# Adding the four quadrants' column sums of a softmax: with six DMAs inside SBUF and VectorE in place of a product on TensorE

## The reference

```python
x_q = einsum('oc,bcn->bno', w_qk, y)
x_k = einsum('oc,bcn->bon', w_qk, x)
x_v = einsum('oc,bcn->bon', w_v, x) + b_v
energy = einsum('bnc,bcm->bnm', x_q, x_k)
attention = softmax(energy, axis=-1)
attention = attention / (1e-07 + attention.sum(axis=1, keepdims=True))   # the column sums
x_r = einsum('bcn,bnm->bcm', x_v, attention)
x_r = relu(einsum('oc,bcn->bon', w_t, x - x_r) + b_t)
return x + x_r
```

## Time and profile before

| | |
|---|---|
| median of three executions | 1884.51 us (1882.46 to 1885.28) |
| the profiled execution, its own time | 1884.3 us |
| its span in the trace | 1882.5 us |
| PE busy | 1875.4 us, 100% |
| VectorE busy | 1464.6 us, 78% |
| ScalarE busy | 1299.8 us, 69% |
| GpSimd busy | 781.4 us, 42% |
| mean granted clock of TensorE | 0.999 of full speed |
| moved by DMA | 101.93 MB, mean 54 GB/s |

### The profile page before, as it was taken

One profiled execution on the slowest core, in us unless ns is written; L12 is line 12 of the kernel. 1 busy time (PEld: TensorE's weight loads), 2 busy tenths in 40 slices (PEclk: granted clock), 3 DMA queues, 4 the chain that ended last, 5 costly groups with the idle time before them and its releaser, 6 DMA issues.

```text
span 1882.5 us, 26348 instructions
## 1 busy us (share of the span) xinstructions
PE 1875.4 (100%) x8948; PEld 1571.5 (83%) x8948; DVE 1464.6 (78%) x1843; ACT 1299.8 (69%) x1793; POOL 781.4 (42%) x420
## 2 busy tenths in 40 slices
PE   9999999999999999999999999999999999999999
PEld 7888888888888888888888888888888888888887
DVE  6888777787777877778777788777787777877777
ACT  6677666677666776667766677666677666776664
POOL 5552444533444324444244452444533444324430
PEclk9999999999999999999999999999999999999999
DMA  3111111011110111111111111111011110111100
GB/s 106 52 39 46 68 67 67 22 49 62 67 67 28 62 45 67 67 45 45 45 67 67 51 38 45 67 67 67 22 50 61 67 67 29 60 45 67 68 12 34
DMA packets 33946, 101.93 MB, mean 54 GB/s; under 512 B 4208, under 2 KB 4976, under 8 KB 33904
## 3 DMA queue, kind: packets, MB, share of 16 engines
q1 hardware_dynamic: 33360, 101.46, 15.0%
q10 hardware_dynamic: 544, 0.00, 0.0%
HBM read 67.90 MB, written 33.55 MB: 54 GB/s over the span
## 4 chain that ended last, share of the span: by engine, by line
PE 99%; ACT 1%; DVE 0%; issue 0%; DVEq 0%
PE pv L685 37%; PE row_b L593 18%; PE row_a L593 14%; PE pv L661 10%; PE row_b L653 5%; PE row_a L653 5%; PE row_b L644 5%; PE row_a L644 5%; PE row_a L692 0%; PE pv L767 0%; PE pv L653 0%; ACT p_sb L300 0%; ACT p_hi L308 0%; PE pv L775 0%; PE row_b L803 0%; DVE colsum L449 0%
## 5 line engine op out<-in xcount | busy, mean ns | idle before, releaser
L198 POOL TENSOR_TENSOR y_lo<-y_raw,y_hi 128x896 fp32r<-128x896 f32 x128 | 279.4, 2206 | 582.3 <-ACT y_hi L262 393.1
L456 DVE SCALAR_TENSOR_TENSOR p_lo<-p_sb,row_inv,p_hi 128x1024 fp32r<-128x1024 f32 x256 | 328.3, 1283 | 94.4 <-ACT p_hi L308 94.4
L291 ACT ACTIVATE ev<-row_b 128x512 f32<-128x512 f32 x384 | 228.4, 595 | 198.4 <-PE row_b L593 198.3
L183 POOL TENSOR_TENSOR x_lo<-x_sb,x_hi 128x1024 fp32r<-128x1024 f32 x63 | 152.5, 2422 | 444.8 <-ACT x_hi L250 444.8
L300 ACT ACTIVATE p_sb<-p_sb,neg_max 128x1024 f32<-128x1024 f32 x256 | 295.0, 1153 | 46.3 <-DVE neg_max L431 42.2
L308 ACT ACTIVATE p_hi<-p_sb,row_inv 128x1024 fp32r<-128x1024 f32 x256 | 292.4, 1142 | 33.4 <-PE pv L685 30.8
L449 DVE SCALAR_TENSOR_TENSOR colsum<-p_sb,row_inv,colsum 128x1024 f32<-128x1024 f32 x224 | 290.3, 1296 | 8.7 <-DVE row_inv L439 0.8
L685 PE MATMUL pv<-p_hi,z_hi 128*128 128x512 f32 x1024 | 274.8, 390 | 0.0
L685 PE MATMUL pv<-p_hi,z_lo 128*128 128x512 f32 x1024 | 273.8, 389 | 0.0
L685 PE MATMUL pv<-p_lo,z_hi 128*128 128x512 f32 x1024 | 273.8, 389 | 0.0
L685 PEld LDWEIGHTS pv<-p_hi,z_hi 128*128 128x128 f32 x1024 | 192.2, 188 | 40.9
(11 more groups left out here) (129 smaller groups left out, 3581.2 us busy)
## 6 DMA issues: line engine op xcount, KB each, us to landing
x_sb<-x SPq DMA_DIRECT2D x64, 512.0 KB, 3.8
out<-res SPq DMA_DIRECT2D x62, 512.0 KB, 2.9
y_raw<-y SPq DMA_DIRECT2D x64, 256.0 KB, 3.6
y_raw<-y SPq DMA_DIRECT2D x32, 512.0 KB, 3.6
out<-res SPq DMA_DIRECT2D x4, 256.0 KB, 2.0
res<-w_qk SPq DMA_DIRECT2D x1, 256.0 KB, 3.6
res<-w_t_T SPq DMA_DIRECT2D x1, 256.0 KB, 7.1
res<-w_v SPq DMA_DIRECT2D x1, 256.0 KB, 7.2
```

Source lines behind the costliest of these rows:

```text
L198: nc.gpsimd.tensor_tensor(y_lo[:, :, cols], y_raw[:, 1:8, cols], y_hi[:, :, cols].bitcast(FP32), ALU.subtract).then_inc(y_lo_done, 1)
L291: nc.scalar.activation(ev[:, to, :], bank_b, ACT.Copy, scale=scale).then_inc(b_copied, 1)
L456: nc.vector.scalar_tensor_tensor(out=p_lo[r][:, :], in0=p_sb[r][:, :], scalar=row_inv[:, j:j + 1], in1=p_hi[r][:, :].bitcast(FP32), op0=AL ...
```

## The change

`same_row`, its making on GpSimd, PE's wait for it, `add_quadrants` and PE's wait for `s_guarded` go. `s_part` becomes four times as wide: `s_part[:, 0, :]` takes the sums of `turn`, and SP, at the end of its part of a batch, waits for them and copies them with six DMAs from SBUF to SBUF, so that slot q of every partition holds the partial sums of the partition 32 q further on, modulo 128. A DMA moves 32, 64 or 96 partitions of 128 bytes each. DVE waits for all six, adds the four slots (128 x 32 from 128 x 128) and goes on as before, with the sum read from SBUF and not from PSUM. `gather_quadrants` also runs for the last batch, ahead of the four stores.

```diff
@@ SP
+            def gather_quadrants(b):
+                sp.wait_ge(s_parted, b + 1)
+                for q in range(1, P // Q):
+                    near, far = P - Q * q, Q * q
+                    sp.dma_start(s_part[0:near, q, :], s_part[far:P, 0, :]).then_inc(s_gathered, DMA)
+                    sp.dma_start(s_part[near:P, q, :], s_part[0:far, 0, :]).then_inc(s_gathered, DMA)
...
                     if not last:
                         load_x(b + 1, 1 - par, t)
+                gather_quadrants(b)
@@ POOL
-            nc.gpsimd.memset(same_row[:, :], 0.0).then_inc(same_row_made, 1)
-            for q in range(P // Q):
-                pool.wait_ge(same_row_made, q + 1)
-                by_quadrant = same_row[:, :].rearrange("p (g i) -> p g i", i=Q)
-                nc.gpsimd.affine_select(out=by_quadrant, in_=by_quadrant, compare_op=ALU.not_equal, fill=1.0,
-                                        base=-Q * q, pattern=[[0, P // Q], [-1, Q]],
-                                        channel_multiplier=1).then_inc(same_row_made, 1)
@@ DVE
-                nc.vector.tensor_reduce(s_part[:, :], turn_buf[:, :].rearrange("p (t q) -> p t q", q=Q), AX.X,
+                nc.vector.tensor_reduce(s_part[:, 0, :], turn_buf[:, :].rearrange("p (t q) -> p t q", q=Q), AX.X,
                                         ALU.add).then_inc(s_parted, 1)
 
             def col_inverse(b):
-                dve.wait_ge(s_done, b + 1)
-                nc.vector.tensor_scalar(s_eps[:, :], row_a[:, 0:N // Q], EPS, None, ALU.add).then_inc(s_guarded, 1)
+                dve.wait_ge(s_gathered, 2 * (P // Q - 1) * DMA * (b + 1))
+                nc.vector.tensor_reduce(s_sum[:, :], s_part[:, :, :].rearrange("p q t -> p t q"), AX.X,
+                                        ALU.add).then_inc(s_summed, 1)
+                dve.wait_ge(s_summed, b + 1)
+                nc.vector.tensor_scalar(s_eps[:, :], s_sum[:, :], EPS, None, ALU.add).then_inc(s_guarded, 1)
@@ PE
-            def add_quadrants(b):
-                pe.wait_ge(s_parted, b + 1)
-                nc.tensor.matmul(row_a[:, 0:N // Q], same_row[:, :], s_part[:, :],
-                                 start=True, stop=True).then_inc(s_done, 1)
...
-                    add_quadrants(b)
                     pv_pass(b, NP - 1, 0, 2)
...
-                    add_quadrants(b)
                     z_half(1 - par, 0)
-                    pe.wait_ge(s_guarded, b + 1)
                     z_half(1 - par, 1)
...
-            pe.wait_ge(same_row_made, P // Q + 1)
```

More of the change, by code:

```diff
@@ L63, in xattn_kernel @@
         eps_wb, bias, neg_bias = sb("eps_wb", [P, KT]), sb("bias", [P, KT]), sb("neg_bias", [P, KT])
-        same_row = sb("same_row", [P, P])
         zeros = sb("zeros", [P, C])
@@ L84, in xattn_kernel @@
         turn_buf = sb("turn_buf", [P, N])
-        s_part, s_eps, s_inv = (sb(name, [P, N // Q]) for name in ("s_part", "s_eps", "s_inv"))
+        s_sum, s_eps, s_inv = (sb(name, [P, N // Q]) for name in ("s_sum", "s_eps", "s_inv"))
+        s_part = sb("s_part", [P, P // Q, N // Q])
         neg_max, row_sum, row_inv = (sb(name, [P, NT]) for name in ("neg_max", "row_sum", "row_inv"))
@@ L102, in xattn_kernel @@
         out_stored = [sem(f"out_stored{mt}") for mt in range(KT)]
-        same_row_made, zeros_made = sem("same_row_made"), sem("zeros_made")
+        zeros_made = sem("zeros_made")
         setup_mm, setup_dve = sem("setup_mm"), sem("setup_dve")
@@ L109, in xattn_kernel @@
         b_done, e_done, row_a_done, row_b_done = sem("b_done"), sem("e_done"), sem("row_a_done"), sem("row_b_done")
-        pv_done, w_done, s_done = sem("pv_done"), sem("w_done"), sem("s_done")
+        pv_done, w_done = sem("pv_done"), sem("w_done")
         x_hi_done, y_hi_done, x_biased = sem("x_hi_done"), sem("y_hi_done"), sem("x_biased")
@@ L120, in xattn_kernel @@
         turned, s_parted, s_guarded = sem("turned"), sem("s_parted"), sem("s_guarded")
+        s_summed, s_gathered = sem("s_summed"), sem("s_gathered")
         s_inverted, s_spread = sem("s_inverted"), sem("s_spread")
```

## The result

The changed kernel takes 1928.43 us (median of four runs, 1926.14 to 1928.65) against 1884.12 us (four runs): the ratio is 1.0232, 95% interval 1.022 to 1.0245. It is 44 us slower, where 5.6 us faster was forecast, and outside the stated range.

The account below looks back on a forecast made before the run. PE, busy for the whole span, was taken to bound the kernel. -7.75 us at 31 boundaries and +2.1 us in the last batch give -5.65 us from 1884.3, so a median of 1878.9 us; range 1876.8 to 1884.3.

Parts of the forecast that it names:

- Removed from PE: At 31 batch boundaries, PE loses the product (0.22 us) and a 0.03 us wait: gain 0.25 us each, 7.75 us.
- Gather on SP: At a boundary, six DMA issues 0.48 us apart and a 2.0 us landing: data there at 945.12, after s_part at 940.67.
- the cover of 5.7: At a boundary, the gain holds while data is in SBUF by 946.37, a landing up to 3.25 us; s_part ends 940.67.
- Rival A: Late at every boundary: with 3.8 us landings s_eps starts 0.45 us later, about 1902 us; chance 0.10.
- the rule on small pieces: Pieces below 512 bytes set the gather's pace: 24 per DMA engine take 5.7 us, about 1945 us; chance 0.02.
- DVE: At a boundary, the new reduction takes 0.29 us, s_eps starts 1.5 us earlier, at 945.45, and p1's 0.03 us wait goes.
- The last batch: No cover there: the gather delays the chain and PE idles some 2.2 us; cost 2.1 us, bounds 0.3 and 4.0.
- rival B in its short form: Last batch: PE's idle time lowers the clock, eight matmuls at 0.2 us more, 1.6 us: 1880.5 us; chance 0.12.
- The rivals: Late data at every boundary (0.10), a clock fall at the end (0.12 for each form), a smaller boundary gain (0.12).
- P: Theory of the follow-ups, not the prediction: a VectorE addition from SBUF to SBUF waits for the running GpSimd instruction.
- a cover of 1.5: At a boundary, spare time from s_eps starting at 945.45 where it started at 946.95: 1.5 us.

## Why the prediction was wrong

Point by point, by its own steps:

- *Removed from PE* (0.22 + 0.03 us, 31 times, 7.75 in all): right. 1.03 us at the boundary after, and 7.8 us in the run without the sum.
- *Gather on SP*: landing 1.8 us where 2.0 was taken, distance of the issues 0.63 us where 0.48 was taken and 0.51 was the upper bound. The bound was wrong, the sum hardly: 4.97 us against 4.45, inside the cover of 5.7. That cover was read at one boundary and taken for all 31; at the first it is 1.25 us shorter, and there the gather is late by some tenths even where nothing waits for GpSimd (the run with the last batch on PE: 0.5 us, once). Rival A and the rule on small pieces did not come about: with the sum in PSUM the same gather gives a kernel that is 3.6 us faster.
- *DVE*: **the step that failed**. I wrote that `s_eps` "then starts at 945.45 where it started at 946.95: 1.5 us earlier" and let the rest of the chain follow at the durations of the kernel before; no row showed the addition with an SBUF source, and none of the terms is a wait for GpSimd. The start was near enough (0.9 us early). But the change moved the source of L470 from PSUM to SBUF, and the duration of 0.19 us, read with a PSUM source, did not hold: 2.32 us at nearly every boundary. The chain came 1.25 us late, PE waited 39.1 us for `z_low`, and the gain of 7.75 us became a loss of 40. The reduction (0.39 where 0.29 was taken) is a trifle beside it.
- *The last batch*: 4.1 us where 2.1 was forecast. 0.5 of the difference is the slower issue, 0.1 the reduction, and 1.5 rival B in its short form: seven steps of 0.42 or 0.43 us between the matmuls of L667 behind 2.25 us of idle time, as the rows of the start had it (there, too, seven such steps, not eight). I had given it a chance of 0.12. It came a second time where I had not looked for it, behind PE's wait at the first boundary.
- *The rivals*: none named GpSimd. Rival A put the loss at PE's wait for `z_low`, which is where it came, but from another cause; that it names the right place is luck. With P as a rival the price would have depended on a few tenths: in the fences above GpSimd is busy over the whole boundary, an instruction of 1.30 us ends just as the one of 2.4 us begins, and `s_eps` comes 0.12 us after that. Up to 2.4 us of waiting against a cover of 1.5 was the range; the measured start fell on its bad end. At the second boundary, where one issue was slow, it came 1.4 us after the start of GpSimd's instruction and waited 1.07.

The trace of before showed the mechanism, in rows that the prediction did not read. In its first microseconds, DVE and then GpSimd:

```profile
10.77 0.68 DVE L557 TENSOR_TENSOR y_raw<-y_raw 128x512 f32<-128x512 f32 x1
11.48 1.67 DVE L559 TENSOR_TENSOR y_raw<-y_raw 128x512 f32<-128x512 f32 x1
13.25 0.69 DVE L561 TENSOR_TENSOR y_raw<-y_raw 128x512 f32<-128x512 f32 x1
```

```profile
10.75 1.84 POOL L234 TENSOR_TENSOR y_raw<-y_raw 128x512 f32<-128x512 f32 x1 [0.99 <-DMA y_raw<-y]
```

The same instruction three times. L559 starts while GpSimd runs and takes 1.67 us, L561 takes 0.69 with GpSimd at rest. L557 starts 0.02 us after GpSimd's and takes 0.68; here it is GpSimd that is held up, 1.84 us where its like takes 1.28 in the batches (L188). And L449, with two inputs in SBUF, had a median of 1.285 us and a maximum of 3.06, at 60.63, beside two instructions of GpSimd that end at 62.6. A maximum far above the median of an instruction that waits for no semaphore is such a sign.

The Trainium skill states the rule, in "SBUF — State Buffer", section "Who interferes with whom": VectorE and GpSimd share a pair of SBUF ports under an exclusive lock, held for a whole instruction; a tensor_scalar between two places in SBUF can take it, an instruction with two SBUF inputs needs it against a GpSimd instruction that reads SBUF, and a tensor_reduce never contends on trn2. The runs agree in each of these: medians of 2.31 us for the tensor_scalar and 2.33 for two inputs, and 0.39 for the reduction. The prediction should have had it as a rival and did not. The Trainium skill bears on the odd number of columns too: "VectorE: DVE Perf Modes", section "What auto-detection actually checks", lets the two-port mode stand where the outermost dimensions of source and destination are both even or are equal, and 33 and 33 are equal; the measured 2.2 us agree.

That the lock is what makes the instruction wait is the page's account. What the runs show is that the addition ends when GpSimd's instruction ends, for one length and for half of it, and that it does not wait with a PSUM source or with GpSimd at rest. Whether another GpSimd operation, one that only writes, would hold it up as well was not tried.

## What to carry to other kernels

When a change moves an operand from PSUM to SBUF, the duration of the instruction is a new one: ask what GpSimd does at that moment, and keep a tensor_scalar or a two-input instruction of a critical chain off SBUF sources, or fold it into a reduction (here a constant in a spare slot). A small gather inside SBUF of six DMAs from one queue takes about 5 us from the producer to the consumer, most of it the issues; it is free where the cover is 5.7 us, late by some tenths where it is 4.5, and paid for where there is none, as in the last batch. Read the cover at each place where the change acts, the first and the last batch too. An idle time of PE of over 2 us can cost more than its own length: 1.5 us on top where the clock falls behind it.

## What was not expected of the hardware

- The issue of a DMA from SBUF to SBUF with 128 bytes for each partition takes SP 0.53 to 0.61 us (median 0.59), and the next follows at 0.57 to 0.65; the y loads take 0.33 and follow at 0.5 us. The landing is 1.7 to 1.8 us for 4, 8 and 12 KB alike.
- At the second boundary, in the last batch ahead of SP's loop, one of the issues takes 1.0 to 1.8 us, in each of the nine traces with the gather; everywhere else the longest is 0.82. Why was not tried.
- Behind 2.10 to 2.47 us of idle time of a PE that had been fully busy, the granted clock fell to the level of 1.2 GHz in eight of eleven places of the traces; in the last batch of the changed kernel it was 0.57 over the 4 us behind it. The 1.1 to 1.3 us at the other boundaries of the changed kernel, and 0.50 us in the last batch with two queues, left the clock at 1.
